# Two transformer-like layers on one core: how K and V reach their spread form, the form of V's product, the pieces of the middle, the sets of the graph attention, and the layout of the output

## The reference, cut to what matters

```
# x 32 x 32 x 128 (batch, token, feature), c = cond_1024 32 x 128, 16 heads of 8 channels
# layer 0: a transformer block with modulation from c
cmod = silu(c) @ w_ada + b_ada          # shift, scale, gate for attention and for the MLP
xm   = ln(x) * (1 + scale) + shift
k, q, v = split(xm @ w_qkv);  w = softmax(q @ k.T / 8) per head;  y = w @ v
x1 = x + gate * (y @ w_proj + b)
x2 = x1 + gate_mlp * (gelu(mod(ln(x1)) @ w_mlp1 + b) @ w_mlp2 + b)
# layer 1: graph attention, two directions d over an adjacency of 32 x 32 x 11 labels
self = [x2, q_or_zero] @ W_self.T + b_self        # q_or_zero is 0 where a row of x2 sums to 0
for d in 0, 1:
    qh = self @ Wq[d].T + bq;  kh = self[:, :20] @ Wk[d].T + bk
    aff = qh . kh / sqrt(8), masked by the adjacency, + label bias
    out_d = softmax(aff) @ self[:, :20], then Wout[d] per head, + bout
return x2 + relu(self + out_0 + out_1)
```

## Time and profile before

| what | value |
|---|---|
| time, median of 3 runs | 119.47 us (117.96 to 120.05) |
| span of the profiled execution, first to last instruction | 116.2 us |
| mean granted TensorE clock, share of full | 0.899 |
| busy: TensorE matmul, VectorE, ScalarE, GpSimd | 93.4, 72.0, 43.2, 44.5 us |

### The profile page before, as it was taken

The page is one execution under the profiler, slowest core; times in us unless marked ns, Lnnn a source line. Parts: engine busy times, 40 slices in busy tenths (PEclk is TensorE's granted clock), DMA queues, the critical chain, the costliest instruction groups (busy, mean ns, idle before and its releaser), DMA issues.

```text
span 116.2 us, 5082 instructions
## 1 busy us (share of the span) xinstructions
PE 93.4 (80%) x2244; PEld 65.9 (57%) x2244; DVE 72.0 (62%) x196; ACT 43.2 (37%) x81; POOL 44.5 (38%) x61
## 2 busy tenths in 40 slices
PE   0499299999929747799699999999999999965550
PEld 0499086656618524565365666576778776643530
DVE  0541974766762647934612527977878796769591
ACT  2700484133402320218605402288595344513110
POOL 7981478999900030223223405400114240300371
PEclk9999955899995997569999999999999999999855
DMA  3999901011112111000000011121101220121003
GB/s 69 312 424 351 282 16 28 23 41 40 38 38 63 48 41 38 6 0 0 0 0 0 0 37 52 24 62 34 57 23 41 52 72 26 31 48 24 10 23 113
DMA packets 6438, 7.51 MB, mean 65 GB/s; under 512 B 1584, under 2 KB 5392, under 8 KB 6288
## 3 DMA queue, kind: packets, MB, share of 16 engines
q1 hardware_dynamic: 5984, 6.67, 18.8%
q10 hardware_dynamic: 432, 0.52, 1.6%
HBM read 4.22 MB, written 0.52 MB: 41 GB/s over the span
## 4 chain that ended last, share of the span: by engine, by line
PE 50%; SPq 25%; DVE 9%; DMA 4%; POOL 4%; issue 3%; ACT 2%; POOLq 0%
SPq L620 9%; SPq L613 7%; PE ps_b L801 6%; PE ps_b L721 5%; SPq L630 5%; SPq L646 5%; PE ps_b L795 5%; PE ps_s L837 5%; PE ps_s L869 4%; PE ps_b L830 3%; PE ps_b L879 3%; DMA Kb<-gated 3%; POOL Kb L576 3%; PE ps_b L768 3%; PE ps_b L904 3%
## 5 line engine op out<-in xcount | busy, mean ns | idle before, releaser
L566 POOL TENSOR_TENSOR home_a<-home_a 128x128 f32<-128x128 f32 x8 | 4.0, 506 | 25.8 <-DVE home_a L1257 25.8
L1019 ACT ACTIVATE PT<-ps_b 120x384 f32<-120x384 f32 x16 | 7.7, 490 | 13.5 <-PE ps_b L879 13.4
L554 POOL TENSOR_TENSOR xT<-gated,xT 128x384 f32<-128x384 f32 (+1 forms) x6 | 5.4, 907 | 16.7 <-DVE gated L1091 16.7
L1022 ACT ACTIVATE PT<-ps_b 128x512 f32<-128x512 f32 x8 | 4.7, 597 | 17.8 <-PE ps_b L882 17.8
L1208 DVE TENSOR_TENSOR E<-ps_s,bias_dir 128x320 f32<-128x320 f32 x16 | 7.8, 488 | 4.1 <-PE ps_s L869 4.0
L904 PE MATMUL ps_b<-Vz,PT 120*32 120x54 f32 (+1 forms) x384 | 7.7, 217 | 2.6 <-DMA Vz<-v_raw 2.3
L693 POOL TENSOR_TENSOR rstd<-var_eps,minus_half 128x2 f32<-128x2 f32 (+2 forms) x8 | 5.6, 708 | 10.4 <-DVE var_eps L1051 10.3
L904 PEld LDWEIGHTS ps_b<-Vz,PT 120*32 120x32 f32 (+1 forms) x384 | 6.1, 115 | 5.4 <-issue 3.5
L837 PE MATMUL ps_s<-ident 128*128 128x128 f32 x24 | 5.4, 423 | 4.6 <-POOL ident L670 4.6
L1246 DVE RECIPROCAL rden<-ps_b 128x32 f32<-128x32 f32 (+1 forms) x13 | 4.3, 336 | 7.7 <-PE ps_b L912 5.0
L957 ACT ACTIVATE hidden<-ps_b,cols 128x384 f32<-128x384 f32 (+1 forms) x12 | 6.4, 544 | 6.9 <-PE ps_b L795 6.7
(11 more groups left out here) (102 smaller groups left out, 206.8 us busy)
## 6 DMA issues: line engine op xcount, KB each, us to landing
w_rest_sb<-in_w_rest SPq DMA_DIRECT2D x1, 1088.0 KB, 7.2
home_a<-in_adj SPq DMA_DIRECT2D x2, 448.0 KB, 10.1
xT<-in_xT SPq DMA_DIRECT2D x1, 512.0 KB, 8.3
home_a<-in_adj SPq DMA_DIRECT2D x1, 512.0 KB, 11.0
Kb<-k_raw SPq DMA_DIRECT2D x16, 30.0 KB, 1.9
Vz<-v_raw SPq DMA_DIRECT2D x12, 36.0 KB, 1.9
Vz<-v_raw SPq DMA_DIRECT2D x8, 50.6 KB
w_ada_sb<-in_w_ada SPq DMA_DIRECT2D x1, 384.0 KB, 4.2
```

Of the source, the lines that this page charges most:

```text
L1019: ins = act.activation(PT[0:KR, key % 3, 0:CH, :], ps[0:KR, 0:CH * P].rearrange("p (j t) -> p j t", t=P), ACT.Exp)
```

## The change

- K of chunks 2, 3, 4 is scaled by one GpSimd multiplication with a mask that writes all four copies (`kmask`), K of chunks 0 and 1 by four masked ScalarE copies each; V of all chunks by `vmask` (GpSimd, chunk 0 on VectorE); k1 of each piece and direction by `k1mask` (six on GpSimd, two on VectorE). No DMA and no clearing is left for Kb0, Vz0 and Kb1. Only v1 goes by DMA still, eight issues for each of four pieces, in a ring of two.
- v and v1 are computed by feature as one matmul (v) or two (v1), and VectorE's 32x32 transpose turns them while it copies them out of PSUM.
- MIDS has four pieces of two groups, in place of three.
- From set 2 on, `scores`, `badd`, `max` and `sub` take two units at once: two groups of layer 0, or both directions of a group of layer 1. `bhead` copies the bias out to four heads (two GpSimd steps). `sub` of six of the eight sets of layer 1 goes to GpSimd.
- x2tok, sbtok, selfb, yb and relu go. y01 is transposed to features (`oT`), `fin1` adds bout and self and `fin2` adds x2 by feature, and the output is stored by feature, in five stores.
- WARM is 6; ident is the first step of GpSimd; w_ada is loaded in two parts, and the bias products of the graph come behind layer 0's attention. ORDER, BANKS and the assignment to engines are new (these lists are left out below).

```diff
-MIDS = [(0, 3), (3, 6), (6, 8)]
-K_MASKED = {0}
-WARM = 24
+MIDS = [(0, 2), (2, 4), (4, 6), (6, 8)]
+V1_RING = 2
+K1_RING = 2
+SETS = [(0,), (1,), (2, 3), (4, 5), (6, 7), (8, 9), (10, 11), (12, 13), (14, 15), (16, 17), (18, 19), (20, 21), (22, 23)]
+FINS = [(0, 2), (2, 4), (4, 6), (6, 7), (7, 8)]
+LOADS_SP = ['cols', 'ada0', 'qkv', 'ada1', 'adj0', 'adj1', 'adj2', 'rest', 'xT']
+K_POOL = {2, 3, 4}
+WARM = 6
...
+        def spread_k(engine, name, h):
+            g0, g1, bs = batches("k", h)
+            for s in fresh(name, ("take", (("k", h), 0)), ("masks", 0)):
+                engine.wait_ge(*s)
+            n = (g1 - g0) * P
+            return engine.tensor_tensor(
+                Kb0[:, :, bs, :].rearrange("p i b s -> p i (b s)"),
+                k0_raw[:, bs, :].rearrange("p b s -> p (b s)").unsqueeze(1).broadcast_to([P, HI, n]),
+                head_mask[:, 1, :].unsqueeze(2).broadcast_to([P, HI, n]), ALU.mult)
...
+        def spread_v(engine, name, h):
...
+            n = (g1 - g0) * UB * HJ * CW
+            return engine.tensor_tensor(
+                Vz0[:, :, bs, :, :].rearrange("p i b j w -> p i (b j w)"),
+                v0_raw[:, bs, :, :].rearrange("p b j w -> p (b j w)").unsqueeze(1).broadcast_to([P, HI, n]),
+                quad_mask[:, :].unsqueeze(2).broadcast_to([P, HI, n]), ALU.mult)
...
+        def spread_k1(engine, name, m, d):
...
+            n = (g1 - g0) * UB * M
...
-                if kind == "v":
-                    w = HJ * C
-                    for b in range(bs.start, bs.stop):
-                        for i in range(HI):
-                            ins = pe.matmul(ps[QUAD * i:QUAD * i + QUAD, (b - bs.start) * w:(b - bs.start + 1) * w],
-                                            xm[:, b, :], w_v0[:, i, :], start=True, stop=True)
-                    return ins
...
+                to = ps[:, 0:DIRS * n].rearrange("p (b d k) -> p b d k", d=DIRS, k=QUAD)
+                for d in range(DIRS):
+                    ins = pe.matmul(to[:, :, d, 0:M], w_v1[:, d, :], selfT[:, bs, 0:M], start=True, stop=True)
...
+                    return dve.transpose(v0_raw[:, bs, :, 0:C].rearrange("p b j c -> p (b j) c"),
+                                         ps[:, 0:nb * S].rearrange("p (r c) -> p r c", c=C))
...
+                    ins = dve.tensor_tensor(E1[:, e_slot(key), 0:u, 0:H * M].rearrange("p u (j x) -> p j u x", x=x),
+                                            ps_s[:, :, 0:u * x].rearrange("p j (u x) -> p j u x", u=u),
+                                            bias.unsqueeze(1).broadcast_to([P, HJ, u, x]), ALU.add)
...
+                    ins = dve.scalar_tensor_tensor(out=outT[:, bs, :], in0=ps, scalar=bout_sum[:, 0:1], in1=selfT[:, bs, :],
+                                                   op0=ALU.add, op1=ALU.add)
...
+                    ins = dve.scalar_tensor_tensor(out=outT[:, bs, :], in0=outT[:, bs, :], scalar=0.0, in1=xT[:, bs, :],
+                                                   op0=ALU.max, op1=ALU.add)
```

More of the change, by code:

```diff
@@ L63 @@
  'exp': 'act',
- 'fetch': 'sp',
+ 'fin1': 'dve',
+ 'fin2': 'dve',
+ 'gbias': 'dve',
  'ident': 'pool',
+ 'k1mask': 'pool',
+ 'kmask': 'pool',
+ 'masks': 'dve',
+ 'max': 'dve',
+ 'mult': 'dve',
+ 'nmr': 'dve',
+ 'pen': 'dve',
+ 'plus1': 'dve',
+ 'recip': 'dve',
  'resid1': 'pool',
@@ L78 @@
  'values': 'pe',
+ 'vmask': 'pool',
  'ya': 'pool',
- 'yb': 'pool',
  'zero': 'pool',
[L82 to L98, removed]
- 'qz': 0,
[L100 to L116, removed]
- ('k', 4): 1,
[L118 to L127, removed]
+ ('apply', 4): 'dve',
@@ new lines @@
+ ('k1mask', (0, 0)): 'dve',
+ ('k1mask', (1, 0)): 'dve',
+ ('resid1', 3): 'dve',
+ ('resid2', 2): 'dve',
+ ('resid2', 3): 'dve',
+ ('shift', (0, 3)): 'pool',
+ ('shift', (1, 0)): 'pool',
+ ('shift', (1, 1)): 'pool',
+ ('shift', (1, 2)): 'pool',
+ ('sub', 7): 'pool',
+ ('sub', 8): 'pool',
+ ('sub', 9): 'pool',
+ ('sub', 10): 'pool',
+ ('sub', 11): 'pool',
+ ('sub', 12): 'pool',
+ ('take', (('cmod', 0), 0)): 'dve',
+ ('take', (('cmod', 1), 0)): 'dve',
+ ('take', (('k', 0), 0)): 'act',
+ ('take', (('k', 0), 1)): 'act',
@@ new lines @@
+ ('take', (('xnT', 3), 0)): 'dve',
+ ('take', (('xnT', 4), 0)): 'dve',
+ ('take', (('yT', 0), 0)): 'act',
+ ('take', (('yT', 1), 0)): 'act',
+ ('take', (('yT', 3), 0)): 'act',
+ ('vmask', 0): 'dve',
+ ('ya', 3): 'dve',
+ ('zero', 'pad'): 'dve'}
+BANKS = {('cmod', 0): 0,
+ ('cmod', 1): 1,
+ 'qz': 0,
+ ('bias', 0): 2,
+ ('xnT', 0): 2,
+ ('q', 0): 3,
+ ('k', 0): 2,
+ ('v', 0): 3,
+ ('xnT', 1): 3,
+ ('q', 1): 2,
+ ('k', 1): 1,
+ ('v', 1): 0,
+ ('xnT', 2): 0,
+ ('q', 2): 3,
+ ('k', 2): 0,
+ ('v', 2): 0,
+ ('xnT', 3): 3,
+ ('q', 3): 2,
+ ('k', 3): 3,
+ ('v', 3): 3,
+ ('xnT', 4): 0,
+ ('q', 4): 0,
+ ('k', 4): 1,
+ ('v', 4): 2,
+ ('turn', 0): 1,
+ ('values', 0): 1,
+ ('turn', 1): 1,
+ ('values', 1): 3,
+ ('turn', 2): 1,
+ ('values', 2): 2,
+ ('turn', 3): 2,
+ ('turn', 4): 2,
+ ('values', 3): 1,
@@ L138 @@
+ ('values', 10): 2,
+ ('turn', 19): 3,
+ ('turn', 20): 2,
+ ('values', 11): 2,
+ ('turn', 21): 3,
+ ('turn', 22): 1,
+ ('values', 12): 1,
+ ('turn', 23): 3,
+ ('yT', 0): 3,
+ ('proj', 0): 3,
+ ('x1tok', 0): 0,
+ ('xn2T', 0): 0,
+ ('mlp1', 0, 0): 3,
+ ('mlp1', 0, 1): 1,
+ ('mlp1', 0, 2): 2,
+ ('mlp1', 0, 3): 0,
+ ('mlp2', 0): 1,
+ ('rowsum', 0): 1,
+ ('self', 0): 0,
+ ('q1', 0, 0): 0,
+ ('k1', 0, 0): 2,
+ ('q1', 0, 1): 0,
+ ('k1', 0, 1): 3,
+ ('v1', 0): 2,
+ ('yT', 1): 2,
+ ('proj', 1): 2,
  ('x1tok', 1): 3,
- ('mlp1', 0, 2): 2,
@@ L299, in kind_of @@
+VALUES_FIRST = {s: [k for stage, k in ORDER if stage == "values" and k in units][0] for s, units in enumerate(SETS)}
+NB1 = max(m1 - m0 for m0, m1 in MIDS) * UB
+MT = NB1 * S
+NS = len(SETS)
 def kind_of(name):
@@ L517, in bank_freed, with scores_freed @@
             return freed_by(earlier[-1]) if earlier else []
+        def scores_freed(s):
+            keys = [k for stage, k in ORDER if stage == "scores"]
+            at = keys.index(s)
+            return [("badd" if layer_of(keys[at - 1]) else "sub", keys[at - 1])] if at else []
         def batches(kind, h):
```

1005 lines of the change are left out of this document (514 added, 491 removed), and 8 rows, old and new, of the table ORDER.

## The result

| | before | after |
|---|---|---|
| time, median (lowest to highest) | 119.76 us (117.96 to 121.11, 4 runs) | 101.55 us (100.61 to 102.83, 4 runs) |
| span of the profiled execution | 116.2 us | 98.9 us, its own time 100.61 |
| mean granted TensorE clock | 0.90 | 0.98 |

The ratio is 0.851 (95% interval 0.837 to 0.865): the change takes 15% off.

The account below looks back on a forecast made before the run. SyncE's DMA issue queue was taken as the bound in two stretches, TensorE from 54 to 92 us. Start 14 + layer 0 22 + rear 62.9 = 98.9 us span; 3.3 added gives 102 us, range 97 to 107 (chance 0.50).

Parts of the forecast that it names:

- The start: Time up to the first scores: 14 us instead of 21.2, between 12 and 17.
- The memset and the transposes: At the start: ident not waiting for a 3.08 us memset and fewer warm transposes, together 7.1 us taken away.
- Layer 0's attention: First scores to layer 0's last values: 22 us in place of 32.7, range 19 to 29.
- SyncE's 36 issues: Layer 0's DMA issues for K and V, 21 us of SyncE, replaced by GpSimd steps and ScalarE work.
- The rear: From layer 0's last values to the end: 53.6 us of TensorE plus 9.3 idle, 62.9 us, between 57 and 70.
- v1 narrow to wide: In the rear: 4.6 us of narrow v1 matmuls on TensorE become 2.3 us of wide ones.
- SyncE ends last by a little: In the rear: v1's queue, 24.6 us long, still ends last, close to TensorE (25 us) and VectorE (28).
- The tail: From the last values to the end: about 7 us, where it was 7.5.
- Rival 1, exclusion: VectorE instructions with two SBUF inputs wait for GpSimd steps, 14 us on VectorE, half on the path: 109 us; chance 0.17.
- Rival 2, latency: Steps of each set run one behind the other, layer 0 stays at 30 us: 110 us; chance 0.10.
- Rival 4, slow masks: GpSimd masks bound layer 0: no gain there above 4.1 ns per element, above 125 us at 6 ns; chance 0.04.
- Rival 5, path not shortened: SyncE's chain was hidden by TensorE work; only the start and removed TensorE work go: 111 us; chance 0.05.

Follow-up runs that it names:

- run 1: The changed kernel with 24 warm transposes again instead of 6: 101.55 us.
- runs 4 to 7: Four kernels built on the kernel before with layer 0's K (chunks 1 to 4) and V masked by GpSimd, differing in clears and adjacency conversions: 122.31, 123.02, 119.64, 113.21 us.
- run 4: The kernel before with K of chunks 1 to 4 and V masked by GpSimd, all else as it was: 122.31 us, ratio 1.025.
- run 6: The kernel before with layer 0's masks, GpSimd's three clears behind the last vmask, and ScalarE's adjacency conversions behind its first K copies: 119.64 us, ratio 1.013.
- Run 3: The changed kernel with K of chunks 2 to 4 and V of layer 0 spread by DMA again, and their clears back on GpSimd: 110.43 us, ratio 0.923.
- run 9: The changed kernel with v and v1 as narrow 32-row matmuls again and plain copies for VectorE's transposes: 110.76 us, ratio 0.924.
- run 2: The changed kernel with four of the eight v1 DMA issues of each piece left out, the buffer filled with ones: 99.77 us, ratio 0.836.
- run 10: The changed kernel with the six graph-stage subtractions given to GpSimd put on VectorE: 101.90 us.
- run 12: The changed kernel with ScalarE's three adjacency conversions ahead of its first K copy: 102.33 us, ratio 0.859.
- runs 3 and 8: Run 3, and the changed kernel with its eight k1mask steps replaced by DMA issues and a clear of Kb1: 123.61 us, ratio 1.040.
- runs 4 and 5: Run 4, and the same kernel with GpSimd's three clears of Kb1 and Vz1 moved behind its last vmask: 123.02 us, ratio 1.041.
- run 7: Run 6 with the three clears taken apart: Kb1's at 2 us, one of Vz1 at 16 us, one behind the first residual: 113.21 us, ratio 0.952.

## Why the prediction was right, point by point

The time (102 against 101.55) and the span (98.9 both) agree better than the terms do. Start, layer 0 and rear were off by +1.2, -2.1 and +0.8 us, which cancel; that the span agrees to the digit is luck. So is part of the last addition: 3.3 us were added to go from the span to the median, and it was 2.65. Only 1.7 to 2.0 us of that stand between the time and the span of one and the same run; the rest comes from the profiled execution being the fastest of its runs, here (100.61) and, by its span, before as well.

- **The start**, 14 forecast, 15.24 measured, in its range. The reason was half right. The memset and the transposes aren't two gains that add up to 7.1 us: with ident early, the transposes cost nothing (run 1). What is shown: in the profile of before cmod's matmuls start behind the transposes at 9.79, and the first transpose of xn at 13.20; after, the first waits for w_ada until 7.46 and the second comes at 9.19, 4.0 us earlier. The other 2.0 us lie between that transpose and the first scores (8.0 us before, 6.05 after), where DMA issues and a landing became ScalarE copies and one mask. The early ident is enough for the 4.0 us: in runs 4 to 7, with the loads as before and all 24 transposes, but without the clears of Kb0 and Vz0, that transpose of xn comes at 8.8 to 9.9. What the forecast overlooked is the adjacency: with ident early, the first scores came at 22.13 where ScalarE stood at its landing (run 4), and at 16.26 where it did not (run 6). And the clock that I thought might be half was 1.00 up to 14 us.
- **Layer 0's attention**, 22 forecast, 19.9 measured. GpSimd's masks took 2.07, 2.11 and 1.15 us on average against 1.86, 2.06 and 1.14 (two of the three K masks took 1.9, the third 2.41, beside VectorE's `vmask`); GpSimd was busy for 18.3 us (18 forecast), TensorE for 20.0 (20 to 23), VectorE for 19.4 (20). What I had wrong is the clock: I had left 2 to 3 us for a reduced one, and it was 1.00. By my own terms that is the 2 us; no run tests it alone. Run 3 shows that the masks, with the clears they save, are the cause of the shorter stage (8.9 us of the time, 5.7 of it in the stage). I had also priced SyncE's 36 issues at 21 us; by my own rows they filled 27.4 us, 0.76 each.
- **The rear**, 53.6 us of TensorE and 9.3 idle forecast; 53.4 and 9.6 measured, by the windows from 36 to 99. The sum is right, one of its parts is not: v1 narrow to wide is 4.6 us to 2.8, not to 2.3. Both v's together are 3.2 us of TensorE, where I had 4.1; in time, run 9 lost 9.2 us, with a lower clock and a later v, and my sum had no term for either.
- **SyncE ends last by a little**: not borne out. The first v1 copy came at 64.0, not 60, and the issues took 0.83 us each instead of 0.77, 26.6 us in all; but TensorE's, VectorE's and SyncE's ends lie so near each other that half the issues gave 1.8 us at most (run 2), and 4.2 us more on VectorE cost nothing (run 10). In run 12, where the first v1 copy came 2.3 us later, the values did wait for the landing, 1.32 us: SyncE is within some 2 us of the bound. Which resource has the last microsecond stays open; no run singles one out.
- **The tail**: 7 forecast, 6.7 measured, counted as the forecast did, from the start of the last values (92.24). The 7.5 us of before were counted from 108.68, and there a second block of values followed:

```profile
110.51 1.35 PE L904 MATMUL ps_b<-Vz,PT 120*32 120x54 f32 x48
```

  From the end of the last values it is 4.3 us before and 4.9 after: this tail did not get shorter. From the first v1 copy to the last values are 28.3 us (28 to 30 forecast); the copy came 4 us later than I had put it, the values 1.2.
- **Rival 1, exclusion**, 109 us: real, and small. The Trainium skill's rule (SBUF — State Buffer, Who interferes with whom) agrees with the trace: VectorE's `ya` of 128 elements took 0.684 us in the changed kernel and 0.292 in run 10, where GpSimd is idle beside it. The mean of 1.160 us for its two `sub` hides the same: one, at 60.37 us, took 1.50 beside the GpSimd mask shown below, the other, at 66.34 with GpSimd idle, 0.82. These two losses are 0.7 and 0.4 us; with `k1mask` (1.08 and 1.33 us) and `vmask` (1.41 against 1.15 on GpSimd) they make some 1.5 to 2 us on VectorE, an estimate, where I had reckoned 14. VectorE's badd and max, the bulk, took 0.81 us, close to the forecast 0.83. The evidence was never one row: in the trace of before `ya` took 0.64 us beside a `sub` at 88.10 as well.

```profile
59.94 1.25 POOL L736 TENSOR_TENSOR Kb<-k_raw,head_mask 128x640 f32<-128x640 f32 x1
...
L704 DVE TENSOR_TENSOR E<-E,neg_max 128x640 f32<-128x640 f32 x2 | 2.3, 1160 | 0.1
...
L709 DVE TENSOR_TENSOR home_a<-home_a 128x128 f32<-128x128 f32 x1 | 0.7, 684 | 0.0
```

- **Rival 2, latency**: run 10 took 0.4 us out of six `sub` links and gained nothing; layer 0 took 19.9 us. It fell.
- **Rival 4, slow masks**: the 1024-element mask took 2.0 ns per element, far from 4.1. (The forecast's sums there were loose: layer 0's 7104 mask elements are 29 us at 4.1 ns, not 33, and 43 at 6 ns, not 48.) But runs 4 and 5 show that the other half of this rival, GpSimd's queue as the new bound, is easily had: 122 to 123 us.
- **Rival 5, path not shortened**: runs 3 and 8 give back 8.9 and 22 us. It fell for the changed kernel. In the old order it is nearer the truth than I had thought: there layer 0's masks shortened the stage by 1.9 us (run 7). These and the 9.2 us of run 9 add to more than the 18 us of the whole change; each undoes one part in an order made for all of them, so they are no shares. The four pieces, the sets of two and the output by feature were undone in no run, so what they give isn't shown.

## What to carry to other kernels

A queue that only issues DMAs can be the bound while its engine counts as idle: look for it in the chain of waits and price it per issue (0.6 to 0.9 us here), not by bytes. Work moved on to an engine has to be costed with everything else in that engine's queue: the same masks were 2.5% slower, and 5% faster once three clears and three conversions had moved out of the way. A wait that looks decisive on a timeline is only a suspect until a kernel without it has run, and one such run isn't enough where two causes overlap: putting the adjacency late gained next to nothing in the kernel before, and 3.4 us where ident was early.
